# The maximum pass of a causal attention kernel on half-array matmuls, two banks at a time

## The reference

```python
q = jnp.einsum('bsd,hde->bhse', x, Wq)      # 16 heads of 64
k = jnp.einsum('bsd,hde->bhse', x, Wk)
v = jnp.einsum('bsd,hde->bhse', x, Wv)
scores = jnp.where(causal, q @ k.T / 8, -inf)
attn = jax.nn.softmax(scores, axis=-1)
y = x + (attn @ v heads side by side) @ Wo  # then layer norm with gamma, beta
x = layernorm(x + y)
x = layernorm(x + ffn(x))                   # silu(x wg) * (x wu) wd, 768 hidden, weights are integers
```

## Time and profile before

| | us |
|---|---|
| median of three runs | 1571.89 (1570.89 to 1572.41) |
| the profiled execution, its own time | 1570.93 |
| its span, first to last instruction | 1569.1 |
| granted TensorE clock, mean over the span | 0.979 |
| first scores matmul to last maximum bank, about | 52 to 1437 |
| TensorE matmul busy | 1480.6 |
| ScalarE, POOL, VectorE busy | 1012.2, 1028.0, 888.5 |

### The profile page before, as it was taken

The page is one execution under the profiler, slowest core; times in us unless marked ns, Lnnn a source line. Parts: engine busy times, 40 slices in busy tenths (PEclk is TensorE's granted clock), DMA queues, the critical chain, the costliest instruction groups (busy, mean ns, idle before and its releaser), DMA issues.

```text
span 1569.1 us, 24096 instructions
## 1 busy us (share of the span) xinstructions
PE 1480.6 (94%) x8576; PEld 1263.2 (81%) x8576; DVE 888.5 (57%) x1816; ACT 1012.2 (65%) x1919; POOL 1028.0 (66%) x976
## 2 busy tenths in 40 slices
PE   4899999999989999999999999999999999999746
PEld 3678888878878888888888888888888888888546
DVE  6655555555545565656556565555656556564246
ACT  3577676767666676766667676666767666676332
POOL 1466666666666675877667585776758576677664
PEclk9899999999999999999999999999999999999869
DMA  3132213221332121221232122231232112221000
GB/s 120 48 115 62 89 52 97 55 83 48 122 115 82 54 89 48 68 82 55 82 108 89 48 56 67 55 109 55 89 91 72 64 54 81 55 62 48 28 1 27
DMA packets 60855, 110.88 MB, mean 71 GB/s; under 512 B 16064, under 2 KB 40896, under 8 KB 60736
## 3 DMA queue, kind: packets, MB, share of 16 engines
q1 hardware_dynamic: 60736, 109.35, 23.2%
HBM read 61.34 MB, written 13.89 MB: 48 GB/s over the span
## 4 chain that ended last, share of the span: by engine, by line
PE 82%; POOL 8%; DVE 7%; issue 2%; ACT 1%; ACTq 0%; POOLq 0%; DVEq 0%
PE bank L646 22%; PE bank L621 15%; PE bank L520 11%; PE bank L593 8%; PE bank L580 7%; PE bank L544 6%; PE bank L692 5%; POOL probs_lo L1107 3%; PE bank L704 3%; PE bank L629 2%; PE bank L600 2%; DVE max_part L937 1%; POOL h_lo L1149 1%; DVE tanh_h L997 1%; DVE tanh_h L994 1%
## 5 line engine op out<-in xcount | busy, mean ns | idle before, releaser
L1107 POOL TENSOR_TENSOR probs_lo<-probs,probs_hi 128x512 fp32r<-128x512 f32 x576 | 738.9, 1289 | 452.9 <-ACT probs_hi L802 452.7
L937 DVE TENSOR_REDUCE max_part<-bank 128x1 f32<-128x512 f32 (+2 forms) x640 | 361.3, 581 | 367.8 <-PE bank L600 236.6
L799 ACT ACTIVATE probs<-bank 128x512 f32<-128x512 f32 x576 | 344.4, 598 | 288.2 <-PE bank L629 194.2
L621 PE MATMUL bank<-Q,K 128*128 128x512 f32 (+3 forms) x1536 | 384.5, 352 | 6.2 <-issue 6.2
L802 ACT ACTIVATE probs_hi<-bank 128x512 fp32r<-128x512 f32 x576 | 342.2, 594 | 0.0
L621 PEld LDWEIGHTS bank<-Q,K 128*128 128x128 f32 x1536 | 253.3, 190 | 34.7 <-issue 7.0
L646 PE MATMUL bank<-probs_hi,VH 128*128 128x512 f32 (+3 forms) x768 | 256.3, 374 | 7.7 <-POOL probs_lo L1107 7.3
L593 PE MATMUL bank<-K,Q 128*128 128x512 f32 (+3 forms) x768 | 248.5, 365 | 4.5 <-DVE max_part L937 2.9
L646 PE MATMUL bank<-probs_hi,VL 128*128 128x512 f32 (+3 forms) x768 | 234.7, 346 | 0.0
L646 PE MATMUL bank<-probs_lo,VH 128*128 128x512 f32 (+3 forms) x768 | 234.4, 346 | 0.0
L593 PEld LDWEIGHTS bank<-K,Q 128*128 128x128 f32 x768 | 136.2, 190 | 33.4 <-DVE max_part L937 8.4
(11 more groups left out here) (135 smaller groups left out, 2342.0 us busy)
## 6 DMA issues: line engine op xcount, KB each, us to landing
Q<-Q SPq DMA_DIRECT2D x64, 256.0 KB, 3.5
K<-K SPq DMA_DIRECT2D x64, 256.0 KB, 3.4
recip_bc<-recip_scratch SPq DMA_DIRECT2D x64, 256.0 KB, 3.4
wh<-w_scratch SPq DMA_DIRECT2D x12, 768.0 KB, 4.3
wl<-w_scratch SPq DMA_DIRECT2D x12, 768.0 KB, 5.9
wo_quad<-wo SPq DMA_DIRECT2D x16, 256.0 KB, 2.9
y<-x SPq DMA_DIRECT2D x4, 1024.0 KB, 5.5
x_tail<-x SPq DMA_DIRECT2D x13, 256.0 KB, 3.0
```

Of the source, the lines that this page charges most:

```text
L621: last = mm(bk[:, at:at + cols], KX[:, n, P * i:P * i + P], QX[:, n, q0:q0 + cols], start=(KX is K1 and at == 0), stop=(KX is K2 and k not ...
L799: A(pe_[:, g % 2, :], stb[g % 2][:, :], ACT.Exp).then_inc(exp_done, 1)
L937: last = V.reduce_max(mp[:, j, c:c + 1], bk[:, at:at + cols], AX.X)
L1107: G.tensor_tensor(pl[:, g % RING, :], pe_[:, g % 2, :], ph[:, g % RING, :].bitcast(F32), ALU.subtract).then_inc(lo_done, 1)
```

## The change

Only the rounded q and the rounded K enter the maximum pass. That is 64 rows, so a bank is made in one half of the array's rows, and an "event" makes two banks, the first in rows 0 to 63 and the second in rows 64 to 127. To have both operands in both halves, K2's copy of rounded K now goes to the other half of the partitions than K1's, and the rest of q and the maximum's row change halves with it. An event stands in every second step (the odd ones of an iteration), nine for a pair of heads; both `mxb` banks are filled, and the next event waits until VectorE has read both. The matmuls of the two halves are issued alternately. The first event of a pair waits for `q_dup` and `k_dup`; therefore `P1_AT` becomes -1, 0, 1, 2 and `dup_k` moves to steps 3 and 21, ahead of `sums` in SyncE's queue. The transposition moves to steps 4, 14, 22, 32, behind pv.

```diff
 MAXB = [
-    [(0, 0, 128), (2, 0, 384)],
-    [(4, 0, 512)],
+    [(0, 0, 128), (2, 0, 384)], [(4, 512, 128), (6, 512, 384)],
+    [(3, 0, 512)], [(7, 512, 512)],
     [(1, 0, 256), (5, 512, 256)],
...
+    [(4, 0, 512)], [(5, 0, 512)], [(6, 0, 512)], [(7, 0, 512)],
 ]
-MDIAG = {0: (0, 3), 2: (1, 3), 3: (0, 3), 4: (3,), 6: (3,)}
+MDIAG = {0: (0, 3), 1: (0, 3), 2: (3,), 3: (3,), 4: (1, 3)}
+MAX_ITEMS = [(0, k) for k in range(9)] + [(1, k) for k in (5, 0, 1, 2, 3, 4, 6, 7, 8)]
+EVENTS = [MAX_ITEMS[2 * e:2 * e + 2] for e in range(9)]
 MAX_LEAD = 13
-T_LEAD = 3
+T_AFTER = [4, 8]
...
-P1_AT = [-1, 1, 2, 3]
+P1_AT = [-1, 0, 1, 2]
...
+        def max_due(g):
+            pair, r = divmod(g + MAX_LEAD, 2 * NS)
+            return (pair, r // 2) if r % 2 == 0 and 0 <= pair < NH // 2 else None
...
-                sp.dma_start(bits(K2[0:E, a, :]), bits(K1[0:E, a, :])).then_inc(k_dup[pair], 16)
-                sp.dma_start(bits(K2[E:P, b, :]), bits(K1[E:P, b, :])).then_inc(k_dup[pair], 16)
+                sp.dma_start(bits(K2[E:P, a, :]), bits(K1[0:E, a, :])).then_inc(k_dup[pair], 16)
+                sp.dma_start(bits(K2[0:E, b, :]), bits(K1[E:P, b, :])).then_inc(k_dup[pair], 16)
...
+            def max_banks(pair, e):
+                r, it = pair % 2, pair // 2
+                if mx_reads(pair, e):
+                    pe.wait_ge(mx_read, mx_reads(pair, e))
+                if e == 0:
+                    pe.wait_ge(q_dup[r], 32 * (it + 1))
+                    pe.wait_ge(k_dup[r], 32 * (it + 1))
+                at = [0, 0]
+                masked = [k in MDIAG for _, k in EVENTS[e]]
+                for t in range(2):
+                    for half, (hd, k) in enumerate(EVENTS[e]):
+                        if t < len(MAXB[k]):
+                            j, k0, cols = MAXB[k][t]
+                            rows = slice(E * half, E * half + E)
+                            KX = K1 if hd == half else K2
+                            n = 2 * r + hd
+                            last = mm(mxb[half][:, at[half]:at[half] + cols], Q1[rows, n, P * j:P * j + P], KX[rows, n, k0:k0 + cols],
+                                      start=(t == 0), stop=not masked[half])
+                            at[half] += cols
...
             def scores(g):
...
-                    pe.wait_ge(k_dup[n // 2], 32 * (h // QH + 1))
+                    pe.wait_ge(proj_lo, 2 * proj_unit(h // QH, n // 2, 3) + 2)
```

More of the change, by code:

```diff
@@ L243, in v_due, with t_due @@
             return it + 1 if s == 0 and 0 <= it < NIT - 1 else None
+        def max_due(g):
+            pair, r = divmod(g + MAX_LEAD, 2 * NS)
+            return (pair, r // 2) if r % 2 == 0 and 0 <= pair < NH // 2 else None
+        def t_due(g):
+            pair, r = divmod(g + MAX_LEAD - 1, 2 * NS)
+            return 2 * pair + T_AFTER.index(r // 2) if r % 2 == 0 and r // 2 in T_AFTER and 0 <= pair < NH // 2 else None
         def p1_due(g, u):
@@ L404, in step @@
                     dup_q(it, 1)
+                if s == 3 and live:
+                    dup_k(it, 1)
                 if s == 3 and it >= 1:
@@ L433, in step @@
                     dup_q(nxt, 0)
+                if s == 21 and nxt < NIT:
+                    dup_k(nxt, 0)
                 if s == 21 and live:
                     sums(QH * it + 1)
[L436 to L437 removed]
                 if s == 23 and live:
@@ L582, in wo_unit @@
                 last.then_inc(wo_mm, 1)
[L584 to L596, removed]
-                    last.then_inc(mx_mm, 1)
@@ L599, in max_mask @@
-            def max_mask(h, k):
-                mm(blocks(mxb[mx_event(h, k) % 2], MDIAG[k]), identb[:, :], maskS[:, 0:len(MDIAG[k]), :],
-                   start=False, stop=True).then_inc(mx_mm, 1)
+            def max_banks(pair, e):
[17 more added lines that the diff above has]
+                            at[half] += cols
+                if not any(masked):
+                    last.then_inc(mx_mm, 1)
@@ L603, in max_transpose, with max_masks @@
+            def max_masks(pair, e):
+                for half, (hd, k) in enumerate(EVENTS[e]):
+                    if k in MDIAG:
+                        last = mm(blocks(mxb[half], MDIAG[k]), identb[:, :], maskS[:, 0:len(MDIAG[k]), :], start=False, stop=True)
+                last.then_inc(mx_mm, 1)
             def max_transpose(h):
-                e = mx_event_t(h)
-                pe.wait_ge(mx_read, e - 1)
+                pe.wait_ge(mx_read, mx_reads_t(h))
                 pe.wait_ge(mx_comb, h + 1)
-                tr(mxb[e % 2][0:TT, 0:P], mc[:, h % 2, :], identf[:, :]).then_inc(mx_mm, 1)
+                tr(mxb[0][0:TT, 0:P], mc[:, h % 2, :], identf[:, :]).then_inc(mx_mm, 1)
@@ L713, in step @@
                     scores(g)
[L714 to L721, removed]
+                due = max_due(g)
+                if due:
+                    max_banks(*due)
                 if 0 <= g < NG and g % NS in DIAG:
                     scores_mask(g)
-                if 0 <= h < NH and k in MDIAG:
-                    max_mask(h, k)
+                if due and any(k in MDIAG for _, k in EVENTS[due[1]]):
+                    max_masks(*due)
                 if 0 <= g - LAG < NG:
                     pv(g - LAG)
+                if t_due(g) is not None:
+                    max_transpose(t_due(g))
                 for n, gset, ts, at in tails(g):
@@ L921, in v_rest, with max_banks @@
                 last.then_inc(v_lo, 1)
[L923 to L944, removed]
+            def max_banks(pair, e):
+                dve.wait_ge(mx_mm, mx_event(pair, e) + 1)
+                for half, (hd, k) in enumerate(EVENTS[e]):
+                    h, bk = 2 * pair + hd, mxb[half]
+                    if 2 * e + half in (0, NS) and h:
+                        dve.wait_ge(mx_comb, h)
+                    if k == PAIRED:
+                        both = mp[:, :, :].rearrange("p j c -> p (j c)")[:, 2:16:9]
+                        V.reduce_max(both, bk[:, :].rearrange("p (a b) -> p a b", a=2), AX.X).then_inc(mx_read, 1)
+                    else:
+                        at = 0
+                        for j, k0, cols in MAXB[k]:
+                            c = k0 // CH
+                            last = V.reduce_max(mp[:, j, c:c + 1], bk[:, at:at + cols], AX.X)
+                            at += cols
+                        last.then_inc(mx_read, 1)
+                    if 2 * e + half in (NS - 1, 2 * NS - 1):
+                        dve.wait_ge(mx_read, mx_reads(pair, e) + half + 1)
+                        if h >= 2:
+                            dve.wait_ge(mx_mm, mx_event_t(h - 2) + 1)
+                        V.reduce_max(mc[:, h % 2, :], mp[:, :, :], AX.X).then_inc(mx_comb, 1)
@@ L1018, in step @@
                         y_add(wo_due(g - 1, u), u)
[L1019 to L1024, removed]
+                if t_due(g - 1) is not None:
+                    max_row8(t_due(g - 1))
+                if max_due(g):
+                    max_banks(*max_due(g))
                 for u in range(4):
```

42 lines of the change are left out of this document (19 added, 23 removed).

## The result

The changed kernel takes 1649.4 us, the median of four runs (1642.7 to 1655.6), against 1571.4 us before: a ratio of 1.050, with a 95% interval from 1.046 to 1.053. It is 78 us slower, outside the range of the prediction, and on the side to which the forecast gave 0.37.

The account below looks back on a forecast made before the run. TensorE, busy 94% of the span, was taken as the bound. Banks -55, changes +17, wait for K +22, VectorE -4, ends +1 gave -19 us: 1570.9 - 19 + 1.0 = 1553 us, range 1522 to 1632.

Parts of the forecast that it names:

- the side to which the forecast gave 0.37: Whole kernel: slower than before by more than 0.2%, chance 0.37.
- The banks, -55 us: Maximum pass: the two half-array matmuls of an event stream side by side, saving 55 us, bounds 24 to 68 or nothing.
- the rival with the late second half: Maximum pass: each second half starts a load later, 0.12 us; saving only 24 us, 1584 us in all; chance 0.15.
- Changing between whole array and halves, 17 us: Around each event on TensorE: 576 changes at 0.03 us each cost 17 us, bounds 0 to 96.
- The other bound: Changes of mode: TensorE finishes what is under way before each, 0.17 us a change, 96 us.
- the rival built on it: Before and after each event: every change empties the array, 96 us instead of 17, 1632 us in all; chance 0.22.
- The first event of a pair, 22 us: First event of each pair of heads: TensorE waits for the copy of K, 22 us together, bounds 10 to 32.
- the step on the load of the row sums: Row sums behind K's copies: up to 3 us later, but only the late event's reading stands behind; cost nothing.
- VectorE, -4 us: Even steps with the tail's gated product: no reduction in front of it, so 4 us less waiting; POOL stays covered.
- Ends, 1 us: Ahead of the first scores: the copies' wait and ten reductions instead of nine for head 0, 1 us more.
- The signs: Trace around events: starts within 0.02 us, next instruction 0.22 to 0.28 us behind, 31 waits for K's copy before L618.
- The gap of the drain: Sign of the drain rival: gaps of 0.17 us or more before an event's first L618 and behind its last.

Follow-up runs that it names:

- x2_same_half: The changed kernel with both banks of an event made in rows 0 to 63, so that they can't stream side by side; 1706.3 us.
- x6_whole_nocopy: The changed kernel with all 128 rows, row sums ahead of K's copies, and the first event waiting for the rest of K, not its copy; 1586.6 us.
- x8_glu_first: The kernel before, with VectorE making the tail's gated product ahead of reading the maximum bank in three steps of an iteration; 1562.8 us.
- x3_sums_first: The changed kernel with SyncE issuing the load of the row sums ahead of the copies of K in steps 3 and 21; 1608.1 us.

## Why the prediction was wrong

**What bounds the kernel.** Right: TensorE, with almost no slack. That is why every wait that the change added came through in full.

**The banks, -55 us.** Right in kind, and a little small. The halves start together, and the rival with the late second half is out. In x2_same_half the pairing is worth 57 us, with a stream of 0.23 us at each event, 66 us, in its rows. The Trainium skill (TensorE: Matmul & The Clock Gate, Part 3) says that the weight load for another row group is pulled ahead; the trace agrees, for the two 64-row loads take 0.19 us together, as long as one of 128 rows.

**Changing between whole array and halves, 17 us.** Wrong. This term was mis-sized, and it is the largest error: 0.03 us a change against 0.13 to 0.14 measured, 0.25 to 0.28 us an event, 72 to 80 us in all. I took the value near the 8-column transposition, and that was no near row: it keeps all 128 rows. The other bound, matmuls that run out before the mode changes, 0.17 us a change and 96 us (576 times 0.17 is 98), was the near one, and the rival built on it was right about its mechanism. In step 3 it is 0.09 us in front of the event, 0.20 behind it, and another 0.10 for weights that are not loaded ahead where an fp32r matmul comes first. The Trainium skill (TensorEngine Tiling (Array Packing), Key Properties) says that a change of mode drains TensorE; the gaps on both sides agree with that. The changes therefore ate the pairing: of the forecast's gain of 38 us from these two terms the three comparisons with whole arrays in the same order leave 3 to 8 us, and part of that lies in the waits and ahead of the first scores.

**The first event of a pair, 22 us.** Wrong, and the second large error: about 66 us by the experiments, 41 for turning SyncE's order round, the clock included, and 25 for taking the copy of K off the event. The copy's own landing was near its estimate: 22.9 us of waits against 22. What failed is the step on the load of the row sums, for which I wrote that the next thing behind it is the reading of the late event, and "Nothing". Between the two stands the negated maximum of the head before, and the event waits for it, because both banks are in use and the transposition's result lies in one of them. In the old order the two banks took turns, and the row sums were ahead of the copies.

**The clock.** Not in the prediction at all. Behind some of the waits of 2.4 to 3.3 us on TensorE the granted clock was 0.50 for 3 to 7 us at a time. This cost some 12 us in iterations 5 to 14, and more in some runs than in others.

**VectorE, -4 us.** Right in kind, and small: the steps with a tail did get shorter, by 0.87 us an iteration in x6_whole_nocopy, some 9 us in the iterations with a tail. It was the one lasting gain, and it could be had alone (x8_glu_first, 9 us). POOL stayed covered, as forecast: TensorE waited 7.7 us for `probs_lo` against 7.3 before.

**Ends, 1 us.** Too small: 5.2 us ahead of the first scores with half arrays, 6.9 with whole ones. I counted one more reduction and not that filling both banks ends the overlap of TensorE and VectorE, where nothing else fills the time.

**The rivals.** The true course was one of them, the drain, plus a wait that none of them had. The drain's 1632 us already counted 22 us of waiting; with the 66 measured and 80 instead of 96 it would have been 1660. That the range missed is due to the wait's bounds, 10 to 32 us, which were worked out from the copies alone. With the sizes that the runs showed the sum is -66 + 80 + 66 - 9 + 5 = 76 us, an estimate, since they come from different runs; 78 were measured.

**The signs.** The two matmuls of an event did start within 0.02 us. The next instruction's start is 0.43 us behind them and not 0.22 to 0.28. The gap of the drain, 0.17 us or more, is there behind the event (0.20) and not in front (0.09). The 31 waits in front of L618 came, but for L974; a copy of K is named once, with 2.2 us.

Left open: how much of the 41 us of x3_sums_first is the wait and how much the clock. By the profiled iterations the wait has some 25 to 30 us of it and the clock 10 to 15; no run holds one of them fixed.

## What to carry to other kernels

A pair of half-array matmuls must stand long enough in its mode to pay for going in and out; here a stay costs 0.25 to 0.28 us and a pair saves 0.23 us, so one pair at a time gains next to nothing (91.47 us an iteration with halves, 91.55 with whole arrays), and the two PSUM banks that the pass has leave no room for more. That two useful pairs in one stay would pay follows from these prices; no run shows it. Where a step is moved past others in a queue, follow each of the moved-past instructions to whoever waits for it, through every engine it passes, before calling it free; here a 4 KB load behind two copies held TensorE through VectorE. And when a new order makes some steps shorter, look for the reason: it may be had without the rest of the change.

## What the runs showed of the hardware that I had not expected

Entering the half array costs 0.09 us after a 512-column matmul, leaving it 0.20 us, and no weight load crosses a change; the price is per stay, the same for two matmuls and for four (0.54 us in front and 0.34 behind in both). The two halves start 0.004 us apart and cost one stream. And idle stretches of TensorE of equal length were followed by the 1.2 GHz clock in some iterations of the changed kernel and by full clock in others: 2.43 us in iteration 9 and 2.75 in iteration 14 by 1.2 GHz, 2.44 in iteration 8 and 2.74 in iteration 13 by full clock.
